# Node update of a graph network: bodies that interleave parts of three groups, and the second norm's affine on turned rows

## The reference, cut to what matters

```
h = x + (attn_out @ O_w + O_b)            # attn_out = x1 * (sum of x1 over edges)
h = layernorm(h, ln1_w, ln1_b)
ffn = relu(h @ f1_w + f1_b) @ f2_w + f2_b
h = layernorm(h + ffn, ln2_w, ln2_b)
gi, gh = h @ gru_w_ih + gru_b_ih, h @ gru_w_hh + gru_b_hh
r, z = sigmoid(gi_r + gh_r), sigmoid(gi_z + gh_z)
n = tanh(gi_n + r * gh_n)
x = layernorm(x + (1 - z) * n + z * h)    # "xmid", no affine
table = [x @ W, x @ W @ a1, x @ W @ a2]   # for the second layer
```

## Time and profile before

| | us |
|---|---|
| median of 3 runs | 2995.52 |
| lowest and highest | 2987.47, 2999.9 |
| the profiled execution | 2991.05 |
| its span, first to last instruction | 2989.3 |
| PE, DVE, ACT, POOL busy in the span | 2688.0, 2495.4, 1354.1, 509.5 |
| node update, first product to last kept copy | 1408.92 to 2044.22 |

### The profile page before, as it was taken

One profiled execution on the slowest core, in us unless ns is written; L12 is line 12 of the kernel. 1 busy time (PEld: TensorE's weight loads), 2 busy tenths in 40 slices (PEclk: granted clock), 3 DMA queues, 4 the chain that ended last, 5 costly groups with the idle time before them and its releaser, 6 DMA issues. The chain is left out here.

```text
span 2989.3 us, 51313 instructions
## 1 busy us (share of the span) xinstructions
PE 2688.0 (90%) x15118; PEld 2018.7 (68%) x15118; DVE 2495.4 (83%) x7353; ACT 1354.1 (45%) x2825; POOL 509.5 (17%) x547
## 2 busy tenths in 40 slices
PE   2699979999999999996888787886999999999996
PEld 1466646666666666664555554554999999999996
DVE  5699979999999999994666565666998989898896
ACT  0233247777777777773323232234543333333332
POOL 5598830000000000000122221120000000000000
PEclk6799989999999999998999999998999999999998
DMA  1111102211222212224021211014555454554543
GB/s 49 49 44 44 40 35 94 93 80 82 93 93 93 86 77 93 93 93 142 25 62 62 62 62 47 15 37 115 131 106 119 87 115 90 110 120 81 120 89 72
DMA packets 405301, 239.24 MB, mean 80 GB/s; under 512 B 325488, under 2 KB 397040, under 8 KB 398864
## 3 DMA queue, kind: packets, MB, share of 16 engines
q1 hardware_dynamic: 383968, 215.53, 26.3%
q10 hardware_dynamic: 19824, 19.32, 2.0%
q0 software_dynamic: 1344, 2.41, 0.3%
HBM read 47.69 MB, written 110.84 MB: 53 GB/s over the span
## 5 line engine op out<-in xcount | busy, mean ns | idle before, releaser
L1369 PE MATMUL b_pagg<-x_parts,b_counts 128*128 128x512 f32 x2401 | 790.4, 439 | 0.0
L1349 DVE TENSOR_SCALAR b_key_hot<-b_keys,b_ends 128x392 bf16<-128x392 f16 x2352 | 752.5, 320 | 0.0
L1749 PE MATMUL d_acc<-d_rows_high,d_weights_high 128*128 128x258 f32 x2401 | 685.4, 285 | 20.3 <-ACT d_y L1683 12.1
L1750 PE MATMUL d_acc<-d_rows_low,d_weights_high 128*128 128x258 f32 x2401 | 679.3, 283 | 0.0
L1751 PE MATMUL d_acc<-d_rows_high,d_weights_low 128*128 128x258 f32 x2401 | 678.4, 283 | 0.0
L1348 DVE TENSOR_SCALAR b_lo_hot<-b_nodes,b_ends 128x128 bf16<-128x128 bf16 x2352 | 594.0, 253 | 5.5 <-POOL b_ends L1316 5.5
L1689 ACT CAST d_weights_high<-d_weights 128x896 fp32r<-128x896 f32 x343 | 322.3, 945 | 534.5 <-PE d_acc L1751 270.6
L1384 PE MATMUL b_pcounts<-b_key_hot,b_lo_hot 128*128 128x392 bf16 x2352 | 528.1, 334 | 15.6 <-DVE b_key_hot L1349 15.6
L1414 ACT CAST b_counts<-b_pcounts 128x392 fp32r<-128x392 f32 x784 | 382.1, 487 | 263.0 <-PE b_pcounts L1384 261.2
L1369 PEld LDWEIGHTS b_pagg<-x_parts,b_counts 128*128 128x128 f32 x2401 | 435.4, 189 | 91.0 <-ACT b_counts L1415 0.7
L1749 PEld LDWEIGHTS d_acc<-d_rows_high,d_weights_high 128*128 128x128 f32 x2401 | 455.5, 190 | 28.8 <-DVE d_weights_low L1615 18.1
(11 more groups left out here) (161 smaller groups left out, 2743.5 us busy)
## 6 DMA issues: line engine op xcount, KB each, us to landing
edge_counts<-b_counts SPq DMA_DIRECT2D x49, 1568.0 KB, 5.1
node_table<-u_table ACTq DMA_DIRECT2D x7, 903.0 KB, 9.0
qx<-in_x SPq DMA_DIRECT2D x49, 128.0 KB, 2.0
x_table<-x_tile ACTq DMA_DIRECT2D x49, 128.0 KB, 1.7
agg<-b_sums SPq DMA_DIRECT2D x49, 128.0 KB, 4.6
u_x<-x_table SPq DMA_DIRECT2D x7, 896.0 KB, 8.8
u_agg<-agg SPq DMA_DIRECT2D x7, 896.0 KB, 11.3
u_x<-in_x SPq DMA_DIRECT2D x7, 896.0 KB, 4.9
```

The costliest lines, as they stand in the source:

```text
L1349: last = nc.vector.tensor_scalar(key1[:, h, q, :], n392[:], ends[:, k, 1, q, j:j + 1], None, ALU.is_equal)
L1369: last = nc.tensor.matmul(pagg[:, o, :], ca[:, o, hi, :], x1_parts[:, hi].rearrange("p m d -> p (m d)"), start=(hi == 0), stop=(hi == TILE ...
L1749: nc.tensor.matmul(acc[:, r, 0:HT], a, high[:, t, :], start=(t == 0), stop=False)
L1750: nc.tensor.matmul(acc[:, r, 0:HT], a, low[:, t, :], start=False, stop=False)
```

## The change

Seven bodies of different kinds take the place of the seven groups: `head` (the first part of group 0), `first`, five `steady`, `last` and `tail`. A steady body b does, in the one order `BODY` for all engines, the GRU rows, last norm and table of group b - 1, f1, f2, second norm and gates of group b, and attention output, first norm and `h1` of group b + 1. The two middle pairs of steady bodies are a loop of two returns. DVE and POOL now follow the same tuple as PE and ACT. `gates` has a fifth entry that holds only the last tanh and combine.

The GRU rows are turned into `mo` banks and read there by DVE (no ACT copy); the table product goes to the `tp` banks. `h1` is kept only as h1 + f2's bias (`ln1_b` and `f2_b` are summed once in `fold_first`), turned in that form, and the bias taken off by ACT while it copies, now in two ACTIVATEs of 128 columns. The second norm's weight and bias are likewise applied by ACT on the turned rows, with one value per partition, so DVE's second norm ends with one `tensor_scalar`. `x` has two buffers, h1's and h2's turned rows have one each, x1 is multiplied in place. `f1` waits once, for all turned rows of the body before, rather than per half.

```diff
+        self.rows = kit.sb("rows", [P, 4, D])
+        self.cols = kit.sb("cols", [P, 3, KC])
...
+    def load_first(self, nc, sp):
         sp.dma_start(self.wo[:], split_rows(self.w["O_w"])).then_inc(self.first_in, 16)
+        for j, name in enumerate(("O_b", "ln1_w", "ln1_b", "f2_b")):
             sp.dma_start(self.rows[:, j, :], self.w[name].partition_broadcast(P)).then_inc(self.first_in, 16)
+        for j, name in enumerate(("f2_b", "ln2_w", "ln2_b")):
+            with nc.allow_non_contiguous_dma("a few hundred values, once"):
+                sp.dma_start(self.cols[:, j, :], self.w[name].rearrange("(m p) -> p m", p=P)).then_inc(self.first_in, 16)
...
+    def fold_first(self, nc, dve):
+        dve.wait_ge(self.first_in, self.FIRST)
+        nc.vector.tensor_tensor(self.rows[:, 2, :], self.rows[:, 2, :], self.rows[:, 3, :], ALU.add).then_inc(self.biased, 1)
+        nc.vector.tensor_scalar(self.cols[:, 0, :], self.cols[:, 0, :], -1.0, None, ALU.mult).then_inc(self.biased, 1)
+        dve.wait_ge(self.biased, self.BIASED)
...
+START = (("attn", 0, 1), ("attn", 1, 1), ("O", 0, 1), ("attn", 2, 1), ("O", 1, 1), ("attn", 3, 1), ("O", 2, 1), ("h1", 0, 1),
+         ("attn", 4, 1), ("O", 3, 1), ("h1", 1, 1), ("attn", 5, 1), ("O", 4, 1), ("h1", 2, 1), ("attn", 6, 1), ("O", 5, 1),
+         ("h1", 3, 1), ("O", 6, 1), ("h1", 4, 1), ("norm", 0, 1), ("h1", 5, 1), ("h1", 6, 1))
+BODY = (("f1", 0, 0), ("gru", 0, -1), ("f1", 1, 0), ("gru", 1, -1), ("f1", 2, 0), ("gru", 2, -1), ("xmid", 0, -1),
+        ("f1", 3, 0), ("gru", 3, -1), ("xmid", 1, -1), ("table", 0, -1), ("f1", 4, 0), ("gru", 4, -1), ("xmid", 2, -1),
+        ("table", 1, -1), ("f1", 5, 0), ("gru", 5, -1), ("xmid", 3, -1), ("table", 2, -1), ("f1", 6, 0), ("gru", 6, -1),
+        ("xmid", 4, -1), ("table", 3, -1), ("f1", 7, 0), ("norm", 0, -1), ("xmid", 5, -1), ("table", 4, -1), ("f2", 0, 0),
+        ("xmid", 6, -1), ("table", 5, -1), ("f2", 1, 0), ("table", 6, -1), ("f2", 2, 0), ("h2", 0, 0), ("f2", 3, 0),
+        ("h2", 1, 0), ("f2", 4, 0), ("h2", 2, 0), ("f2", 5, 0), ("h2", 3, 0), ("f2", 6, 0), ("h2", 4, 0), ("norm", 0, 0),
+        ("gates", 0, 0), ("h2", 5, 0), ("h2", 6, 0), ("attn", 0, 1), ("attn", 1, 1), ("O", 0, 1), ("attn", 2, 1),
+        ("gates", 1, 0), ("O", 1, 1), ("attn", 3, 1), ("O", 2, 1), ("h1", 0, 1), ("attn", 4, 1), ("O", 3, 1), ("h1", 1, 1),
+        ("gates", 2, 0), ("attn", 5, 1), ("O", 4, 1), ("h1", 2, 1), ("attn", 6, 1), ("O", 5, 1), ("h1", 3, 1),
+        ("gates", 3, 0), ("O", 6, 1), ("h1", 4, 1), ("norm", 0, 1), ("h1", 5, 1), ("h1", 6, 1), ("gates", 4, 0))
+END = (("gru", 0, -1), ("gru", 1, -1), ("gru", 2, -1), ("xmid", 0, -1), ("gru", 3, -1), ("xmid", 1, -1), ("table", 0, -1),
+       ("gru", 4, -1), ("xmid", 2, -1), ("table", 1, -1), ("gru", 5, -1), ("xmid", 3, -1), ("table", 2, -1), ("gru", 6, -1),
+       ("xmid", 4, -1), ("table", 3, -1), ("norm", 0, -1), ("xmid", 5, -1), ("table", 4, -1), ("xmid", 6, -1),
+       ("table", 5, -1), ("table", 6, -1))
+PLANS = {"head": START, "first": tuple(s for s in BODY if s[2] >= 0), "steady": BODY,
+         "last": tuple(s for s in BODY if s[2] <= 0), "tail": END}
+TURNED = ("attn", "h1", "h2", "xmid", "table")
+SUMMED = ("O", "f2", "gru")
...
+    def tp_free(self, step):
+        at = self.turned.index(step)
+        return self.turned0 + (at - 1 if at else 0)
...
+def update_bodies(eng, run):
+    run(Body("head", -1, 1, 0, 0))
+    run(Body("first", 0, 0, 2 * GROUP, GROUP))
+    with eng.Fori(0, (GROUPS - 3) // 2) as i:
+        for k in range(2):
+            b = 2 * i + 1 + k
+            run(Body("steady", b, (1 + k) % 2, b * TP, b * MO))
+    run(Body("steady", GROUPS - 2, (GROUPS - 2) % 2, (GROUPS - 2) * TP, (GROUPS - 2) * MO))
+    run(Body("last", GROUPS - 1, (GROUPS - 1) % 2, (GROUPS - 1) * TP, (GROUPS - 1) * MO))
+    run(Body("tail", GROUPS, GROUPS % 2, (GROUPS - 1) * TP + 3 * GROUP, (GROUPS - 1) * MO + 2 * GROUP))
...
+                def load(dst, src, g, sem):
+                    sp.dma_start(dst, src[group_rows(g), 0:D].rearrange("(n p) d -> p n d", p=P)).then_inc(sem, 16)
+                def body(B):
+                    if not any(s[2] == 1 for s in PLANS[B.kind]):
+                        return
+                    g = B.group(1)
+                    wait_over_zero(sp, tp_full, B.turned0)
+                    load(at[:], x1, g, x1_in)
+                    if B.kind != "head":
+                        sp.wait_ge(attn_ready, GROUP * g)
+                    load(agt[:], agg, g, agg_in)
+                    if B.kind == "steady":
+                        sp.wait_ge(mo_out, B.mo_full(("gru", GROUP - 1, -1)))
+                    load(xt[:, (B.odd + 1) % 2], x, g, x_in)
+                    if B.kind == "head":
                         weights.load_rest(nc, sp)
...
+                    elif what == "f1":
+                        if n == 0:
+                            pe.wait_ge(tp_out, B.turned0)
+                            if B.kind == "first":
+                                pe.wait_ge(weights.rest_in, weights.REST)
...
+                def evacuate_columns(B, s, dst, scale, bias):
+                    act.wait_ge(tp_full, B.tp_full(s))
+                    for k in range(KC):
+                        last = nc.scalar.activation(dst[:, k, :], tp[:, B.tp_bank(s), tile(k)], ACT.Identity,
+                                                    scale=scale[:, k:k + 1] if scale is not None else 1.0, bias=bias[:, k:k + 1])
+                    last.then_inc(tp_out, 1)
...
+                    elif what == "h1":
+                        if B.kind == "head" and n == 0:
+                            act.wait_ge(weights.biased, weights.BIASED)
+                        evacuate_columns(B, s, h1T[:, :, tile(n)], None, weights.cols[:, 0, :])
...
+                        evacuate_columns(B, s, h2T[:, :, tile(n)], weights.cols[:, 1, :], weights.cols[:, 2, :])
...
+                    if what == "attn":
+                        if n == 0:
+                            if B.kind == "head":
+                                pool.wait_ge(weights.first_in, weights.FIRST)
+                            pool.wait_ge(x_in, 16 * g + 16)
+                            wait_over_zero(pool, mo_out, B.summed0)
+                        nc.gpsimd.tensor_tensor(xb[:, n, :], xt[:, (B.odd + 1) % 2, n, :], weights.rows[:, 0, :], ALU.add) \
+                            .then_inc(xb_ready, 1)
+                    elif what in WHICH:
+                        k = WHICH[what]
+                        pool.wait_ge(var_ready, B.mo_full(s))
+                        nc.gpsimd.tensor_tensor(rs[:, k, n:n + 1], ve[:, k, n:n + 1], c["half"][:], ALU.pow).then_inc(rstd_ready, 1)
...
+                def finish(B, s):
+                    what, n, dg = s
+                    g, k = B.group(dg), WHICH[what]
+                    mean, rstd = mv[:, k, n, 0:1], rs[:, k, n:n + 1]
+                    if what == "O":
+                        dve.wait_ge(normed, upto(g, n))
+                        if B.kind != "head":
+                            dve.wait_ge(tp_full, B.tp_full(("h2", n, 0)))
+                        dve.wait_ge(rstd_ready, B.mo_full(s))
+                        nc.vector.scalar_tensor_tensor(out=hb[:, n, :], in0=h[:, n, :], scalar=rstd, in1=weights.rows[:, 2, :],
+                                                       op0=ALU.mult, op1=ALU.add).then_inc(hb_ready, 1)
+                        return
+                    rows, ready = (hb, h2_ready) if what == "f2" else (xm, xm_ready)
+                    dve.wait_ge(rstd_ready, B.mo_full(s))
+                    nc.vector.tensor_scalar(rows[:, n, :], rows[:, n, :], mean, rstd, ALU.subtract, ALU.mult).then_inc(ready, 1)
...
+                def new_gate(g, q):
+                    half, m = q // KC, q % KC
+                    cols = slice(half * HALF, (half + 1) * HALF)
+                    dve.wait_ge(hf_full, HF * g + 2 * FC + 4 * q + 4)
+                    dve.wait_ge(gates, GAT * g + 2 * q + 1)
+                    nc.vector.scalar_tensor_tensor(out=nT[:, m, cols], in0=hf[:, 3, 0:HALF], scalar=weights.bhh[:, 4 + m:5 + m],
+                                                   in1=rT[:, m, cols], op0=ALU.add, op1=ALU.mult).then_inc(reset_applied, 1)
+                    dve.wait_ge(reset_applied, GQ * g + q + 1)
+                    nc.vector.tensor_tensor(nT[:, m, cols], nT[:, m, cols], hf[:, 2, 0:HALF], ALU.add).then_inc(new_pre, 1)
+                def body(B):
+                    waiting = []
+                    for s in PLANS[B.kind]:
+                        what, n, dg = s
+                        g = B.group(dg)
+                        if what == "attn":
+                            if n == 0:
+                                dve.wait_ge(x1_in, 16 * g + 16)
+                                dve.wait_ge(agg_in, 16 * g + 16)
+                            nc.vector.tensor_tensor(at[:, n, :], at[:, n, :], agt[:, n, :], ALU.mult).then_inc(attn_ready, 1)
```

(38 more changed lines are left out.)

358 lines of the change are left out of this document (142 added, 216 removed), and 3 rows, old and new, of the table UPDATE_STEPS.

## The result

The changed kernel takes 3030.75 us (median of 4 runs, 3024.42 to 3038.4) against 2995.73: 1.0122 times as long, interval 1.0109 to 1.0135. The profiled execution took 3031.47, its span 3029.7. Predicted were 3032 and the side "slower".

What follows compares the result with a forecast made beforehand. PE waiting for DVE (68.3 us work of 88.8 a group). Head 33 + first 84.6 + steady 472 + return 6 + last 59.8 + tail 21 = 676.4 against 635.3, plus 1.2 at the start: 3032 us, 8 in 10 2985 to 3060.

Steps and rivals of the forecast that it cites:

- four seams: PE without a gates step: A, B, C between gates 0 to 3, D before f1 0; 19.3 of 47.2 us lost.
- the signs that it named: Bodies 92 to 97 us, seven DVE waits of 2 to 3.4, clock near 0.5 at gates starts, f1 0 5.7 late.
- Body at full clock: Steady body: 47.2 us from gates 0's end to f1 0, 41.2 for the rest; 88.4, 0.4 less than before.
- Clock, 5 a body: Gaps in the seams lower PE's clock: three falls taken at 1.7 us each, 5 a body; bounds 0 and 6.8.
- That is 1.7 us lost, in each of the seven groups: Kernel before: after PE's 3.3 us wait the clock fell, eight table passes took 3.59 us instead of 1.9.
- POOL, 1 a body: POOL's x + bias between O tiles slows four DVE products or finishes: 0 to 2.2 us a body, 1 taken.
- Loop return, 6: One return inside the steady bodies, meeting the loads of that body's start: 3 to 8 us, 6 taken.
- Head, first body, ends: Stage's ends: head 33 us, first body 84.6, last 59.8, tail 21; and 1.2 at the start for loads.
- DVE's saving is worth nothing, the ACTIVATEs 0.3: Some 5.7 us removed from DVE falls in its waits: nothing; ACT's two ACTIVATEs add 0.3 in seam D.
- The clock did not hold: Rival: the clock holds through the seams and POOL disturbs nothing; 2995 us, no change; 15%.
- half clock did not last through the seams: Rival: half clock lasts through B and C and into the head; about 5 us a body more, 3063; 10%.
- PE is fed in time: Rival: products and finish reach PE while gates still run; 2887 us for all, more likely 2965; 13%.

Runs made afterwards that it cites:

- The first experiment: The changed kernel with DVE making all seven products for the next group in one run before gates 0; 2938.1 us, 0.981 of the kernel before.
- the filled kernel: The changed kernel with 12 to 24 dummy transposes on PE ahead of each of seven turns it waits for in a body; 2998.74 us, 1.001.
- the kernel without a loop: The changed kernel with its four middle bodies written out instead of a loop of two returns; 3015.86 us, 1.0065 of the kernel before.
- the affine on rows: The changed kernel with the second norm's weight and bias applied by DVE on rows again, one ACT copy for h2; 3049.34 us, 1.0164.
- the filled kernel before: The kernel before with 24 dummy transposes in PE's wait behind the last gate of each group; 2996.55 us, 1.0017 of the kernel before.
- the filled pair: The changed kernel with dummy transposes, second norm's affine on ACT (2998.74 us, 1.001) or back on DVE's rows (3001.4 us, 1.0031).
- the paired plan: The changed kernel reordered: products before gates 0, O steps paired behind gates, f1 split; 2896.72 us; affine on DVE's rows 2890.09; that with steady bodies written out 2883.23.

## Why the prediction was right, point by point

*What bounds it.* Right. The sum was built on PE waiting in four seams behind DVE's queue. Priced from zero at the end of gates 0 (1659.88 us in the rows above), PE was to be through attn 2 at 6.5 us, end gates 1 at 12.6 and start attn 3 at 16.8; measured are 6.8, 12.8 and 16.9. Of the signs that it named, the bodies (92 to 97 us) came, and so did f1 0 5.7 us after gates 3 (5.7). Of the seven long waits in this body six are put to products (1.5 to 3.1 us; attn 1 follows attn 0 at once) and one, of 2.6, to the finish in seam D. The first experiment shows the cause.

*Body at full clock.* Predicted 88.4; measured 87.3 without a loop (86.7 less the dummies' share), 88.8 inside it. Right by its parts too: the seams were priced at 6.5, 9.4, 7.3 and 5.7 us and take 6.35 (7.0 with the dummies), 9.1, 7.1 and 5.4; the rest was priced at 41.2 outside the gates steps 1 to 3, and takes 40.7.

*Clock, 5 a body.* As an average right (5.3 by the filled kernel, about 6 with what the dummies cost), as a mechanism too tidy. I counted falls per seam; the kernel without a loop shows that like seams cost 2.7 us in one body and 6.9 in the next (90.0 and 94.2 against 87.3; 0.65 more in each against 86.7), and with the affine on rows one body took 9.8 more than the next. The Trainium skill (TensorE: Matmul & The Clock Gate, What's actually happening) was cited for speaking against a sparse plan; the filled kernel, 32 us faster with 124 transposes more in a body, agrees with it.

*The base for it was misread.* The step "That is 1.7 us lost, in each of the seven groups" fell: the filled kernel before is not faster. The passes were slower, but DVE's chain beside them was longer. So at full clock the change starts from 88.7, not from the 87.1 which that step implied. Written out, its plan gains 1.4 us a group by structure (2.0 without the dummies' share), inside the loop next to nothing, and the clock takes 5 to 6 us away. The 1.7 stood in the sum only as the price of a fall in a seam, where PE does bound; there it did no harm.

*POOL, 1 a body.* The size was nearly right, the place wrong, so 0 in the time. None of the 49 products and 49 finishes of the first norm was longer. Two other ops were, in each of six bodies, a second norm's finish (0.81 us instead of 0.40) and the middle operation of a combine:

```profile
1655.91 1.45 POOL L780 TENSOR_TENSOR u_x_plus_bias<-u_x,rows 128x256 f32<-128x256 f32 x2
1655.97 0.81 DVE L821 TENSOR_SCALAR u_h_plus_bias<-u_h_plus_bias,u_mean_var,u_rstd 128x256 f32<-128x256 f32 x1 [0.44 <-POOL u_rstd L785]
1685.08 1.03 DVE L831 TENSOR_TENSOR u_rT<-u_rT,u_zT 128x448 f32<-128x448 f32 x1
```

That is 0.4 + 0.4 us a body, but both lie while PE works on a gates step (gates 0 from 1653.87, gates 2 from 1682.46), which hides them.

*Loop return, 6.* Too small. DVE stood 5.77 us for no releaser where it had stood 2.81:

```profile
1718.24 0.42 DVE L873 TENSOR_TENSOR u_xmid<-u_mo,u_x 128x256 f32<-128x256 f32 x1 [5.77 <-issue]
```

With the clock held the body of the return costs 9. As it was, it took 104.75 against 92.2 to 95.4 (cut at the copies 100.7 against 92.1 to 96.9), so with half-clock stretches in every body its own share can't be read from one window. That this is the return is shown by the filled kernels; why DVE stands longer there than before is open.

*Head, first body, ends.* Head 33.06 (33), last and tail 83.9 (80.8), first body 79.5 (84.6: at a clock of 0.97 it had the least of the half-clock stretches, where I gave it a full 5). What lies outside the stage is 1.1 us longer (1.2), but this hit says little: over the executions profiled here that time lay between 2351.7 and 2360.7 us.

*The total.* The five steady bodies with the return take 478.1 us where 478 were priced, and that hides two misses: four plain ones are 93.3 on average instead of 94.4, and the return's is 11.4 longer than they are instead of 6. With 5 too much for the first body and 3 too little at the end, the stage is 674.6 instead of 676.4. Besides, the 42 us were put on the profiled execution (2991.05) to get 3033, and 3032 was then given for the median; on the median of 2995.7 they would give 3038. The side, the mechanism and the size of the parts are right; that the total came within 1.3 us of the measured median is luck.

*DVE's saving is worth nothing, the ACTIVATEs 0.3.* Nearly right for this plan: by the filled pair the saving, less what the second ACTIVATE costs, is worth 3 us in the stage, 6 by the ratios. It isn't a property of the edit: in the old order ACT's form costs 1.3 us a group, in the paired plan about 1.7 a body. The ACTIVATEs' durations were taken as 0.35:

```profile
L700 ACT ACTIVATE u_h2T<-u_tp,cols 128x128 f32<-128x128 f32 x98 | 38.7, 454 | 58.6 <-PE u_tp L599 58.6
L700 ACT ACTIVATE u_h1T<-u_tp,cols 128x128 f32<-128x128 f32 x98 | 30.5, 363 | 70.6 <-PE u_tp L599 70.6
```

363 ns with a bias alone, 454 with scale and bias.

*The rivals.* The clock did not hold, and half clock did not last through the seams (in the body shown, attn 3, O 2 and h1 0 pass at full speed behind a wait of 3.05 us). "PE is fed in time" did not come by itself; the first experiment built a part of it, and its 2938 lies between the two prices given, 2887 for all and 2965 for a quarter. That the paired plan (2883 to 2897) lands near the 2887 is no test of that price, since it moves f1, O and h1 as well.

## What to carry to other kernels

In a plan that all engines follow in one order, look for the small operation that another engine waits for (here a product of 0.42 us) and stands last behind work which itself waits; moving it ahead added no work and was worth 93 us. A stretch at half clock is a cost only if PE sets the end there, so see who waits behind it before you price it. And when two variants differ by a few us a body, compare bodies at equal granted clock, or hold the clock with filler, before you give the difference to the edit.

## What the runs showed of the hardware that was not expected

*Whether DVE or POOL waits goes by who began first.* In the kernel before, POOL's seven additions ran in one piece and a DVE op with two inputs in SBUF that came into them took 1.03 us instead of 0.48. In the changed kernel DVE's product begins first (1676.26 us, 0.42 long, as always), and POOL's addition beside it is the long one, 0.94 instead of the 0.72 that it takes alone:

```profile
1666.35 0.72 POOL L780 TENSOR_TENSOR u_x_plus_bias<-u_x,rows 128x256 f32<-128x256 f32 x1
1676.32 0.94 POOL L780 TENSOR_TENSOR u_x_plus_bias<-u_x,rows 128x256 f32<-128x256 f32 x1
```

It is so throughout the stage: 22 products overlap one of POOL's additions, all began first and took 0.41 or 0.42 us, and the 12 DVE ops that were longer, named under *POOL* above, all began after it. POOL has time there. That is why the products stayed short. The Trainium skill (SBUF — State Buffer, Who interferes with whom) says that the order of issue decides who blocks; the trace agrees, and I had taken from the page only that the two disturb each other.

*The same steps at two clocks.* Like bodies, with DVE's busy time equal within 0.05 us, lasted 90.08 and 94.32 us at clocks of 0.96 and 0.91, and in another kernel 98.80 and 89.02 us at 0.88 and 0.98; with dummies in the gaps neighbours were equal to 0.01 us in the first of them and within 1.1 us in the second. The runs don't show what in the timing of the gaps decides it.

*Writing the loop out* (it ran twice, with two bodies each time, and so returned once) was worth 12 us of 643 in the stage with the clock held, 8 us by the ratios. The body where it returned is 9 longer than its neighbours, and these are 1.4 longer than the ones written out; in the paired plan they are not (72.1 to 72.4 and 72.2), and why is open.
